# Decay sums of a Mamba-2 scan: spread over the partitions by a DMA through memory, for three chunks in four

## The chip, the cores and the metric

One core of a Trainium2 chip. Its engines are TensorE (PE), VectorE (DVE), ScalarE (ACT), GpSimd (POOL) and SyncE (SP), which here only issues transfers. They run side by side and wait for each other by semaphores. The metric is the time of one execution on the device in microseconds, the median of several.

## The reference

A macaron block on 2048 tokens of width 512: half a feed-forward layer with int4 weights and a low-rank part, a Mamba-2 mixer with a gated feed-forward layer behind it, and again half the feed-forward layer. The change touches the scan of the mixer alone (4 heads of 128, state 128, chunks of 128 tokens):

```python
a = (dt * A).reshape(B, c, Q, H).transpose(0, 1, 3, 2)
cs = jnp.cumsum(a, axis=-1)
Ldec = jnp.where(tri, jnp.exp(cs[..., :, None] - cs[..., None, :]), 0.0)
att = jnp.einsum('bchqn,bchkn->bchqk', Cc, Bc) * Ldec
Yd = jnp.einsum('bchqk,bchkp->bchqp', att, Xdt)
dec_end = jnp.exp(cs[..., -1:] - cs)
Yo = jnp.einsum('bchqn,bchpn,bchq->bchqp', Cc, prev, jnp.exp(cs))
```

`cs`, the decay sums of a chunk, is 4 heads by 128 tokens. It is wanted twice: as a column (a token to a partition) and as a row that is the same on all 128 partitions.

## The kernel before

The program is written out engine by engine; nothing reorders it. There are 16 chunks (`NCH`) of 128 tokens in 4 stretches (`NS`) of 4 (`CH`); chunk c is number j = c mod 4 of stretch i. The middle part, from about 80 to 330 us, runs `step(c)` for c = 0 to 15 on each engine. A step interleaves four things: the first feed-forward layer of chunk c + 8 (`f`, `hi0`, `lo0`, `hi1`, `lo1`, `x1_stats`), the projections and the convolution of the next stretch (`proj`, `slot_a`, `slot_b`, `taps`, `silu`), the scan of chunk c and the first half of that of chunk c + 1, and the output product and residual of chunk c (`w`, `renorm`, `residual2`, `square`). Each stretch has ten projection blocks, dealt out to the steps by `SLOTS = ((0, 1, 2), (3, 4), (5, 6, 7), (8, 9))`.

The scan of a chunk, in the lines of the profile:

- Once a stretch PE forms the sums by a triangular matmul (`csm`, L2022 and L2023), as a column and as rows of 80 partitions in PSUM. DVE (`cut_decay`, L1396 to L1406) takes the negated column into `ncs` and cuts the rows into three bf16 parts in `cs_b`, so that a bf16 matmul gives them back whole.
- For each chunk PE (`s1`) issues four selection matmuls (`decay_rows`, L2047), one a head, which put that head's sums on all 128 partitions, in PSUM bank `B_CS`; then two transposes of x and B (L2041).
- ACT (`scan_ecs`, L817) takes their exponential into `ecs`, copies the transposes into `tm` (`scan1`, L811), and some work later forms the decay matrix (`scan_decay`): four Abs of the row plus the negated column (L826) and an exponential (L829). `scan2` (L835) scales x by `wv`, which DVE makes out of the decay (L1411).
- DVE multiplies decay and product (L1420), POOL masks the triangle and adds the skip (L554, L556), PE multiplies on (`s2_diag` L2066, `s2_state` L2075, `s2_inner` L2083), DVE gates the result (`gate_y`, L1430) and advances the state (L1437), and PE applies the output weights (`w`, L2093).

ACT issues the first half of chunk c + 1 at the start of step c: `scan_ecs`, `scan1`, then convolution blocks and `hi0`, `hi2`, then `scan_decay`, `hi1`, `scan2`. PE's products for the projections and the feed-forward layer share three PSUM banks in turn, each freed by whoever read it last; DVE's `gate_y(c)` frees nothing but is what `w(c)` waits for.

SP's queue is served in order, and an issue whose semaphore isn't there holds up all behind it. Before the loop it does, for c = 4 to 7, the transpose of chunk c's normalised rows (`t1`, L444, which waits for DVE's `lo1(c)`), the load of x for chunk c + 4 (`next_x`, L401) and the transpose for the feed-forward layer (`t0`); then the first pair of gate and up weights (`load_pair`, L436 to L440). In step c it does `t0(c + 9)`, `t2(c - 1)`, `t1(c + 8)`, `next_x(c + 8)`, as far as they exist.

Of the kernel before, what the change touches and what calls it, by code (L numbers as in the profile page):

```python
# [27 lines left out]
def build(nc, x_in, w_in_t, conv_w, conv_b, a_log, d_skip, dt_bias, w_out_t, ln1_w, ln2_w,  # L28
# [23 lines left out]
    with ctx:  # L52
# [209 lines left out]
        e_x_bn, e_x_var, e_x_rstd, e_x_scale, e_n0_hi, e_n0_lo, e_n0_tr = (  # L262
            sem(n) for n in "e_x_bn e_x_var e_x_rstd e_x_scale e_n0_hi e_n0_lo e_n0_tr".split())
        e_n0T, e_ffn, e_x1, e_x1_bn, e_x1_var, e_rms1, e_hn_scale = (
            sem(n) for n in "e_n0T e_ffn e_x1 e_x1_bn e_x1_var e_rms1 e_hn_scale".split())
# [18 lines left out]
        e_scx, e_wscale, e_dsx, e_descale, e_c_var, e_c_rstd, e_c_scale = (  # L284
            sem(n) for n in "e_scx e_wscale e_dsx e_descale e_c_var e_c_rstd e_c_scale".split())
        e_cn_hi, e_cn_lo, e_cffn, e_c_bias, e_out, e_c_bn = (
            sem(n) for n in "e_cn_hi e_cn_lo e_cffn e_c_bias e_out e_c_bn".split())
# [2136 lines left out]
```

## Time and profile before

| | us |
|---|---|
| median of 3 runs | 765.47 |
| lowest and highest | 765.44, 765.92 |
| the profiled execution | 766.1 |
| its span, first to last instruction | 764.4 |
| granted TensorE clock | 1.00 |

An engine's row in a timeline gives the start and the length; "[1.22 <-PE PS L2047]" says that the engine had been idle for 1.22 us and what released it. Matmuls are pipelined and their lengths overlap: what one costs is the distance to the next start. The chain that ended last is followed back from the end, at each step to what released an instruction or to the instruction before it on its engine.

### The profile page before, as it was taken

The numbers are of one execution on the slowest core, as the hardware profiler recorded it, in microseconds if no ns is written. First come the engines' busy times: TensorE is split into PE (matmuls) and PEld (weight loads), VectorE is DVE, ScalarE is ACT, GpSimd is POOL, SyncE is SP. The second block draws the span as 40 slices with busy tenths as digits, with TensorE's granted clock in tenths as the row PEclk, the third lists the DMA queues.
The fourth block names the chain that finished last, engine by engine and source line by source line (L and its number), as shares of the span: only waits on it lengthen the run. The fifth ranks groups of instructions, "written<-read, shape, count | busy, mean of one in ns | idle before, by whom it ended". The sixth has DMA issues, their size and how long they took to land.

```text
span 764.4 us, 10533 instructions
## 1 busy us (share of the span) xinstructions
PE 752.1 (98%) x3406; PEld 351.1 (46%) x3406; DVE 627.6 (82%) x1236; ACT 446.9 (58%) x881; POOL 338.5 (44%) x392
## 2 busy tenths in 40 slices
PE   8999999999999999999999999999999999999998
PEld 3444544454554444444443444444444444444443
DVE  7799778878878979878899978878878878767994
ACT  4867867677786676643645556456456456444441
POOL 5631544663442389765413343243243243224574
PEclk9999999999999999999999999999999999999999
DMA  8833634553331122420520833733733733443564
GB/s 302 198 72 80 148 71 89 107 101 70 69 68 26 33 42 65 87 56 1 137 42 15 179 70 70 165 69 70 166 70 69 164 72 69 79 74 71 120 168 137
DMA packets 95413, 71.85 MB, mean 94 GB/s; under 512 B 65232, under 2 KB 72400, under 8 KB 95360
## 3 DMA queue, kind: packets, MB, share of 16 engines
q0 software_dynamic: 17280, 31.46, 23.0%
q1 hardware_dynamic: 77600, 39.66, 20.1%
q8 instruction: 27, 0.44, 0.2%
q14 instruction: 26, 0.21, 0.1%
q10 hardware_dynamic: 480, 0.07, 0.1%
HBM read 20.32 MB, written 4.19 MB: 32 GB/s over the span
## 4 chain that ended last, share of the span: by engine, by line
PE 66%; DVE 19%; ACT 7%; issue 4%; POOL 2%; DMA 2%; ACTq 0%; POOLq 0%; DVEq 0%
PE PS L1968 59%; PE PS L2093 3%; DVE raw L1455 3%; DVE st L1290 1%; DVE stage L1455 1%; DVE state L1437 1%; DMA x_t<-hb 1%; DVE xs L1387 1%; PE PS L2066 1%; PE PS L2075 1%; ACT pre L885 1%; PE PS L2083 1%; PE PS L2058 1%; ACT raw L886 1%; DVE n_p L1369 1%
## 5 line engine op out<-in xcount | busy, mean ns | idle before, releaser
L713 POOL DMA_DIRECT2D xs<-x x59 | 51.1, 866 | 151.5 <-ACT x L1160 137.5
L1968 PE MATMUL PS<-h,w_in 128*128 128x512 f16 x480 | 108.7, 379 | 0.2 <-issue 0.2
L1968 PE MATMUL PS<-h,x_t 128*128 128x512 f16 x408 | 94.0, 379 | 0.0
L1968 PEld LDWEIGHTS PS<-h,w_in 128*128 128x128 f16 x480 | 46.9, 98 | 65.3 <-issue 15.3
L1968 PE MATMUL PS<-n_T,stage 128*128 128x512 f16 x288 | 71.5, 379 | 0.0
L1160 ACT ACTIVATE x<-PS,d_d 128x512 f32<-128x512 f32 x59 | 40.2, 682 | 39.3 <-PE PS L1968 38.7
L1968 PEld LDWEIGHTS PS<-h,x_t 128*128 128x128 f16 x408 | 39.5, 98 | 48.5 <-issue 2.3
L522 POOL TENSOR_TENSOR r<-mv,mhalf 128x1 f32<-128x1 f32 (+1 forms) x32 | 29.5, 922 | 67.9 <-DVE mv L1294 53.8
L713 POOL DMA_DIRECT2D xs<-n x29 | 25.3, 871 | 70.5 <-ACT n L1160 61.1
L1968 PE MATMUL PS<-pre,stage 128*128 128x512 f16 x192 | 49.3, 379 | 0.0
L1130 ACT ACTIVATE xds<-tm,dgh 128x512 f32<-128x512 f32 x24 | 17.3, 722 | 53.3 <-DVE tm L1897 53.3
L1968 PEld LDWEIGHTS PS<-n_T,stage 128*128 128x128 f16 x288 | 28.2, 98 | 34.0 <-ACT x L1160 0.3
L1968 PE MATMUL PS<-w_ffn,raw_gu 128*128 128x512 f16 x192 | 43.2, 379 | 0.0
L1455 DVE SCALAR_TENSOR_TENSOR raw<-pre,cw,raw 128x512 f32<-128x512 f32 x36 | 28.0, 777 | 9.7 <-ACT raw L886 9.4
L1968 PE MATMUL PS<-raw,x_t 128*128 128x512 f16 x144 | 34.7, 379 | 0.4 <-DVE Ld L1850 0.4
L1968 PE MATMUL PS<-w_in,x_t 128*128 128x512 f16 x144 | 34.8, 379 | 0.0
L1968 PE MATMUL PS<-h,n 128*128 128x512 f16 x144 | 33.2, 379 | 0.3 <-DVE n L1535 0.3
L1160 ACT ACTIVATE n<-PS,d_d 128x512 f32<-128x512 f32 x29 | 19.8, 684 | 23.2 <-PE PS L1968 22.5
L2093 PE MATMUL PS<-w_out,stage 128*128 128x512 f32 x64 | 29.3, 600 | 0.3 <-DVE stage L1430 0.2
L1968 PEld LDWEIGHTS PS<-w_ffn,raw_gu 128*128 128x128 f16 x192 | 18.8, 98 | 22.7 <-DMA raw_gu<-h2n_p 0.3
L1968 PEld LDWEIGHTS PS<-pre,stage 128*128 128x128 f16 x192 | 18.7, 98 | 22.7 <-ACT x L1160 0.3
L2093 PE MATMUL PS<-w_out,raw 128*128 128x512 f32 x64 | 29.0, 595 | 0.1
(319 smaller groups left out, 1821.7 us busy)
## 6 DMA issues: line engine op xcount, KB each, us to landing
xs<-x POOLq DMA_DIRECT2D x75, 256.0 KB, 3.3
xs<-n POOLq DMA_DIRECT2D x29, 256.0 KB, 3.2
x_t<-x_in SPq DMA_DIRECT2D x16, 256.0 KB, 3.0
x_t<-hb POOLq DMA_DIRECT2D x16, 256.0 KB, 3.8
out<-x_t SPq DMA_DIRECT2D x16, 256.0 KB, 2.3
raw_gu<-gate_t SPq DMA_DIRECT2D x7, 512.0 KB, 4.4
raw_gu<-up_t SPq DMA_DIRECT2D x7, 512.0 KB, 6.5
raw_d<-down_t SPq DMA_DIRECT2D x7, 512.0 KB, 7.3
```

Of the source, the lines that this page charges most:

```text
L522: return po.tensor_tensor(dst, src, mhalf[:, 0:src.shape[-1]], ALU.pow)
L713: po.dma_start(chunk_of(xs, c), d_tmps[d % 3], accum_op=ALU.add).then_inc(s_acc[d % 3], 16)
L885: ac.activation(pre[:, w, NTAP - 1:], src, ACT.Copy)
L886: last = ac.activation(xbc[i % 2][:, b, :], src, ACT.Identity, scale=cw[:, b, NTAP - 1:NTAP], bias=cb[:, b:b + 1])
L1130: ac.activation(th_s[ab], u4 if ab else c11, ACT.Tanh, scale=dgh[:, p % 2:p % 2 + 1]).then_inc(e_tanh_g, 1)
L1160: ac.activation(d_tmps[d % 3], bank(d_bank(d)), ACT.Copy, scale=d_d[:, p % 3:p % 3 + 1]).then_inc(e_ev, 1)
L1290: link(ve.bn_stats(stat, src), e_link, base + 1)
L1369: return ve.tensor_tensor(pair_[:, 1, :], src, pair_[:, 0, :], ALU.subtract)
L1387: link(ve.scalar_tensor_tensor(chunk_of(xs, c), bank(b), 0.5 / ACT_SCALE if c < NF else d_f[:, :], x_t[:, j, :], ALU.mult, ALU.add), e_x1, ...
L1455: ins = ve.scalar_tensor_tensor(xbc[i % 2][:, b, :], pre[:, w, k:k + ST], cw[:, b, k:k + 1], xbc[i % 2][:, b, :], ALU.mult, ALU.add)
L1968: ins = pe.matmul(out_, lhs(a, b, k), rhs(a, b, k), start=first and n == 0, stop=last and n == len(todo) - 1)
L2093: last = pe.matmul(bank(b), y[:, h, (c % CH) * P:(c % CH + 1) * P], w_out[:, h, :], start=h == 0, stop=h == H - 1)
```

## The change

For chunks with j = 1, 2 and 3 the row on all partitions comes from memory. DVE copies the 16 rows of a stretch as they are in PSUM into `cs_f` (first thing in `cut_decay`); SP writes them to a tensor `cs_d` in memory (`cs_store`) and for each such chunk reads the 512 numbers back, the same for every partition, into one buffer `cs_all` (`cs_rows`). ACT's `scan_ecs` and `scan_decay` read `cs_all` in SBUF for these chunks and wait for the transfer. For j = 0 the selection matmuls stay. `cs_all` is free for chunk c when the Abs of the chunk that used it before are done (`e_gap`). In the last three steps `t2(c - 1)` moves behind `cs_rows`. To make room for semaphores, pairs that followed each other on one engine now count on that engine's common semaphore (`chain` in place of `link`); these instructions and their order stay.

```diff
+        cs_f = sb("cs_f", [CH * H, P])
+        cs_all = sb("cs_all", [P, H, P])
+        cs_d = nc.dram_tensor("cs_d", (NS, CH, 1, H * P), F32, kind="Internal").ap()
...
+            def cs_store(i):
+                sp_.wait_ge(e_cs_f, i + 1)
+                sp_.dma_start(cs_d[i, :, 0, :].rearrange("j (h t) -> (j h) t", h=H), cs_f[:, :]).then_inc(s_csd, 16)
+
+            def cs_rows(c):
+                i, j = divmod(c, CH)
+                if j > 0:
+                    sp_.wait_ge(s_csd, (i + 1) * 16)
+                    if c > 1:
+                        sp_.wait_ge(e_gap, c if j > 1 else c - 1)
+                    sp_.dma_start(cs_all[:, :, :].rearrange("p h t -> p (h t)"), cs_d[i, j, :, :].broadcast_to([P, H * P])).then_inc(s_cs, 16)
...
+                if c == CH + 1:
+                    cs_store(0)
+            cs_rows(1)
             sp_.wait_ge(e_cv, NPC)
             load_pair(0)
...
-                if c > 0:
+                if 0 < c <= 3 * CH:
                     t2(c - 1)
                 if a < NCH:
                     t1(a)
                     next_x(a)
+                if c + 2 < NCH:
+                    cs_rows(c + 2)
+                if c % CH == 2 and c + 2 < NCH:
+                    cs_store(c // CH + 1)
+                if c > 3 * CH:
+                    t2(c - 1)
...
+            def rows_ready(c, j):
+                if j == 0:
+                    ac.wait_ge(e_cs, c // CH + 1)
+                else:
+                    ac.wait_ge(s_cs, (c - c // CH) * 16)
+
+            def rows_of(j):
+                return cs_all[:, :, :] if j else heads(B_CS)
...
-                ac.wait_ge(e_cs, c + 1)
+                rows_ready(c, j)
                 if c - 1 > 0:
                     ac.wait_ge(e_state, c - 1)
-                ac.activation(ecs[:, j % 2, :, :], heads(B_CS), ACT.Exp).then_inc(e_ecs, 1)
+                ac.activation(ecs[:, j % 2, :, :], rows_of(j), ACT.Exp).then_inc(e_ecs, 1)
...
                     ve.wait_ge(e_cs_col, i + 1)
+                    if i > 0:
+                        ve.wait_ge(s_csd, i * 16)
+                    ve.tensor_copy(cs_f[:, :], rows[0:NT]).then_inc(e_cs_f, 1)
                     ve.tensor_copy(cs_b[0:K_CS, :], rows[0:K_CS]).then_inc(e_cs_cut, 1)
...
                 if j == 0:
                     pe.wait_ge(e_cs_b, i + 1)
-                if c > 0:
-                    pe.wait_ge(e_gap, c)
-                decay_rows(B_CS, j).then_inc(e_cs, 1)
-                if j == 0:
+                    if c > 0:
+                        pe.wait_ge(e_gap, c - CH + 1)
+                    decay_rows(B_CS).then_inc(e_cs, 1)
                     pe.wait_ge(e_xbc, i * CB + 2)
...
-            def stats(src, mv, stat, e_link, base, e_ve):
-                link(ve.bn_stats(stat, src), e_link, base + 1)
-                link(ve.bn_aggr(mv[:, 0:2], stat), e_link, base + 2)
+            def stats(src, mv, stat, e_ve):
+                chain(ve.bn_stats(stat, src))
+                chain(ve.bn_aggr(mv[:, 0:2], stat))
```

On SP, where the loop is entered (from the transpose of chunk 6's rows on; `h` is the tensor that the transposes fill, x_t the loads of x), before:

```order
L444 DMA_TRANSPOSE h<-hn_p 128x8x128 [waits e_hn_lo]
L401 DMA x_t<-x_in 128x512 [waits e_x1]
L444 DMA_TRANSPOSE n_T<-n_p 128x8x128 [waits e_ffn,e_n0_lo]
L444 DMA_TRANSPOSE h<-hn_p 128x8x128 [waits e_hn_lo]
L401 DMA x_t<-x_in 128x512 [waits e_x1]
L436 DMA raw_gu<-gate_t 128x4x256 [waits e_cv]
L437 DMA raw_gu<-up_t 128x4x256
L440 DMA raw_d<-down_t 128x2x512
L444 DMA_TRANSPOSE n_T<-n_p 128x8x128 [waits e_ffn,e_n0_lo]
```

and now:

```order
L470 DMA cs_d<-cs_f 16x128 [waits e_cs_f]
L447 DMA_TRANSPOSE h<-hn_p 128x8x128 [waits e_hn_lo]
L404 DMA x_t<-x_in 128x512 [waits e_x1]
L447 DMA_TRANSPOSE n_T<-n_p 128x8x128 [waits e_ffn,e_n0_lo]
L447 DMA_TRANSPOSE h<-hn_p 128x8x128 [waits e_hn_lo]
L404 DMA x_t<-x_in 128x512 [waits e_x1]
L478 DMA cs_all<-cs_d 128x512 [waits s_csd]
L439 DMA raw_gu<-gate_t 128x4x256 [waits e_cv]
L440 DMA raw_gu<-up_t 128x4x256
L443 DMA raw_d<-down_t 128x2x512
L447 DMA_TRANSPOSE n_T<-n_p 128x8x128 [waits e_ffn,e_n0_lo]
```

The store of the first stretch's sums stands first in this piece; the read of chunk 1's rows stands behind the last transpose and load ahead of the loop, and the weight pair follows it.

On ACT, in step 0, from the last product of the prologue to the decay of chunk 1, before:

```order
L901 ACTIVATE th<-PS,d_ih 128x512 [waits e_proj,e_sz]
L817 ACTIVATE ecs<-PS 128x512 [waits e_cs]
L811 ACTIVATE tm<-PS 128x256 [waits e_xB_tr]
L768 ACTIVATE n<-x_t,b,r 128x512 [waits s_n0T,e_x_scale]
L768 ACTIVATE n_p<-x_t,b,r 128x512
L826 ACTIVATE Ld<-PS,ncs 128x128 [waits e_S,e_cs,e_ncs]
L826 ACTIVATE Ld<-PS,ncs 128x128 x3
L829 ACTIVATE Ld<-Ld 128x512 [waits e_gap]
```

and now:

```order
L930 ACTIVATE th<-PS,d_ih 128x512 [waits e_proj,e_sz]
L846 ACTIVATE ecs<-cs_all 128x512 [waits s_cs]
L831 ACTIVATE tm<-PS 128x256 [waits e_xB_tr]
L788 ACTIVATE n<-x_t,b,r 128x512 [waits s_n0T,e_x_scale]
L788 ACTIVATE n_p<-x_t,b,r 128x512
L855 ACTIVATE Ld<-cs_all,ncs 128x128 [waits e_S,s_cs,e_ncs]
L855 ACTIVATE Ld<-cs_all,ncs 128x128 x3
L858 ACTIVATE Ld<-Ld 128x512 [waits e_gap]
```

Nothing moved; the exponential and the Abs read another buffer and wait for a transfer in place of PE.

On PE, around `s1(2)`, between the projection blocks of step 0 and the feed-forward product of step 1, before:

```order
L1968 MATMUL PS<-h,w_in 128x512 [waits e_conv]
L1968 MATMUL PS<-h,w_in 128x512 x11
L2047 MATMUL PS<-cs_b,sel_b 128x128 [waits e_gap]
L2047 MATMUL PS<-cs_b,sel_b 128x128 x3
L2041 MATMUL PS<-ident,stage 128x128 [waits e_spx,e_xB_T]
L2041 MATMUL PS<-ident,stage 128x128
L1968 MATMUL PS<-w_ffn,n_T 128x512 [waits e_x2,s_n0T]
L1968 MATMUL PS<-w_ffn,n_T 128x512 x11
L2066 MATMUL PS<-S,tm 128x512 [waits e_y,e_xB_T,e_SD]
```

and now:

```order
L2000 MATMUL PS<-h,w_in 128x512 [waits e_conv]
L2000 MATMUL PS<-h,w_in 128x512 x11
L2072 MATMUL PS<-ident,stage 128x128 [waits e_spx,e_xB_T]
L2072 MATMUL PS<-ident,stage 128x128
L2000 MATMUL PS<-w_ffn,n_T 128x512 [waits e_x2,s_n0T]
L2000 MATMUL PS<-w_ffn,n_T 128x512 x11
L2096 MATMUL PS<-S,tm 128x512 [waits e_y,e_xB_T,e_SD]
```

Four matmuls are gone from between the blocks; the same at the other eleven chunks with j > 0.

## Rows read from the trace of the kernel before

**Rows 1.** The page: busy us by engine; share of the chain by engine.

```profile
PE 752.1 (98%) x3406; PEld 351.1 (46%) x3406; DVE 627.6 (82%) x1236; ACT 446.9 (58%) x881; POOL 338.5 (44%) x392
...
PE 66%; DVE 19%; ACT 7%; issue 4%; POOL 2%; DMA 2%; ACTq 0%; POOLq 0%; DVEq 0%
```

**Rows 2.** Chain that ended last, 55 to 345 us: start, length in us, what.

```profile
106.13 0.68 ACT raw L886
...
147.31 3.70 PE PS L2093 x8
...
173.91 0.68 ACT stage L886
...
281.63 1.12 PE PS L2066 x2
```

**Rows 3.** Selection matmuls: line 2047 by form, then PE's timeline (start, length).

```profile
L2047 PE MATMUL PS<-cs_b,sel_b x64: 217/218/222, 79.2 to 306.5; 80*128 80x128 bf16 x64
...
119.75 0.39 PE L2047 MATMUL PS<-cs_b,sel_b 80*128 80x128 bf16 x4
...
119.97 0.39 PE L2041 MATMUL PS<-ident,stage 128*128 128x128 f32 x2
```

**Rows 4.** SP's timeline, 60 to 340 us: start, time of issue.

```profile
85.88 1.23 SPq L444 DMA_TRANSPOSE h<-hn_p  x1
...
87.16 1.06 SPq L401 DMA_DIRECT2D x_t<-x_in  x1
...
152.25 0.57 SPq L401 DMA_DIRECT2D x_t<-x_in  x1
```

**Rows 5.** DMA issues, KB, us to landing: 88 to 90 us; page; hb's load.

```profile
raw_gu<-gate_t SPq DMA_DIRECT2D x1, 512.0 KB, 4.4
...
x_t<-x_in SPq DMA_DIRECT2D x1, 256.0 KB, 3.6
...
x_t<-x_in SPq DMA_DIRECT2D x16, 256.0 KB, 3.0
...
DMA to landing us min/median/max: 5.7/5.7/5.7
```

**Rows 6.** ACT's timeline: start, length, [idle before <-releaser].

```profile
86.55 0.58 ACT L817 ACTIVATE ecs<-PS 128x512 f32<-128x512 f32 x1
...
92.41 0.81 ACT L788 ACTIVATE hn<-xs,b,r 128x512 f32<-128x512 f32 x1 [1.92 <-POOL b L525]
...
101.86 0.21 ACT L884 ACTIVATE pre<-hist 128x3 f32<-128x3 f32 x1 [0.27 <-PE PS L1968]
...
104.68 0.60 ACT L817 ACTIVATE ecs<-PS 128x512 f32<-128x512 f32 x1 [1.22 <-PE PS L2047]
...
154.60 0.59 ACT L817 ACTIVATE ecs<-PS 128x512 f32<-128x512 f32 x1
...
160.71 0.82 ACT L788 ACTIVATE hn<-xs,b,r 128x512 f32<-128x512 f32 x1 [1.55 <-POOL b L525]
```

**Rows 7.** DVE's timeline around chunk 1, and PE's row of its w.

```profile
97.08 2.33 DVE L1455 SCALAR_TENSOR_TENSOR raw<-pre,cw,raw 128x512 f32<-128x512 f32 x3 [0.67 <-ACT raw L886]
...
103.26 0.75 DVE L1455 SCALAR_TENSOR_TENSOR raw<-pre,cw,raw 128x512 f32<-128x512 f32 x1 [1.82 <-ACT raw L886]
...
106.83 0.75 DVE L1455 SCALAR_TENSOR_TENSOR raw<-pre,cw,raw 128x512 f32<-128x512 f32 x1 [1.17 <-ACT raw L886]
...
112.82 0.74 DVE L1430 SCALAR_TENSOR_TENSOR stage<-PS,d_ih,stage 128x512 f32<-128x512 f32 x1
...
113.62 3.70 PE L2093 MATMUL PS<-w_out,stage 128*128 128x512 f32 x8
```

**Rows 8.** Lines 1396 and 829 by form; PE's longest wait, 55 to 335 us.

```profile
L1396 DVE CAST cs_b<-PS x4: 276/277/281, 62.2 to 263.8; 80x128 bf16<-80x128 f32 x4
...
L829 ACT ACTIVATE Ld<-Ld x16: 629/630/632, 82.3 to 310.6; 128x512 f32<-128x512 f32 x16
...
PE PS L2066 <- POOL S L556: 1.0, 1, 1.0
```

More of the change, by code:

```diff
@@ L261, in build @@
         e_aexp = sem("e_aexp"); e_wf = sem("e_wf"); e_dve = sem("e_dve"); e_pool = sem("e_pool")
[L262 to L265, printed above, removed]
+        e_x_var, e_x_scale, e_n0_hi, e_n0_lo, e_n0_tr = (
+            sem(n) for n in "e_x_var e_x_scale e_n0_hi e_n0_lo e_n0_tr".split())
+        e_n0T, e_ffn, e_x1, e_x1_var, e_hn_scale = (
+            sem(n) for n in "e_n0T e_ffn e_x1 e_x1_var e_hn_scale".split())
         e_hn_hi, e_hn_lo, e_proj, e_conv, e_hist = (
@@ L283, in build @@
             sem(n) for n in "e_gated_lo e_down e_acc e_w_gu0 e_w_gu1d e_w_hi e_fold e_mk".split())
[L284 to L287, printed above, removed]
+        e_scx, e_wscale, e_descale, e_c_var, e_c_scale = (
+            sem(n) for n in "e_scx e_wscale e_descale e_c_var e_c_scale".split())
+        e_cn_hi, e_cn_lo, e_cffn, e_c_bias, e_out, = (
+            sem(n) for n in "e_cn_hi e_cn_lo e_cffn e_c_bias e_out".split())
         W_HI_G = [4 * p - 1 for p in range(NP)]
@@ L528, in ln0 @@
                 po.wait_ge(e_x_var, c + 1)
-                rsqrt(r0[:, c:c + 1], mv0[:, c, 2:3]).then_inc(e_x_rstd, 1)
-                po.wait_ge(e_x_rstd, c + 1)
+                chain(rsqrt(r0[:, c:c + 1], mv0[:, c, 2:3]))
                 shift(b0[:, c:c + 1], r0[:, c:c + 1], mv0[:, c, 0:1]).then_inc(e_x_scale, 1)
@@ L540, in ln1_chain @@
                 po.wait_ge(e_x1_var, c + 1)
-                rsqrt(r1[:, c, :], mv1[:, c, 2:4]).then_inc(e_rms1, 1)
-                po.wait_ge(e_rms1, c + 1)
+                chain(rsqrt(r1[:, c, :], mv1[:, c, 2:4]))
                 shift(b1[:, c, :], r1[:, c, :], mv1[:, c, 0:1]).then_inc(e_hn_scale, 1)
@@ L732, in c_norm @@
                 po.wait_ge(e_c_var, c + 1)
[L733 to L734 removed]
+                chain(rsqrt(rC[:, c:c + 1], mvC[:, c, 2:3]))
                 shift(bC[:, c:c + 1], rC[:, c:c + 1], mvC[:, c, 0:1]).then_inc(e_c_scale, 1)
@@ L825, in scan_decay @@
                 for h in range(H):
-                    last = ac.activation(Ld[:, h, :], heads(B_CS)[:, h, :], ACT.Abs, bias=ncs[:, s, j * H + h:j * H + h + 1])
+                    last = ac.activation(Ld[:, h, :], rows_of(j)[:, h, :], ACT.Abs, bias=ncs[:, s, j * H + h:j * H + h + 1])
                 last.then_inc(e_gap, 1)
@@ L2042, in s1, with decay_rows @@
                 last.then_inc(e_xB_tr, 1)
-            def decay_rows(b, j):
+            def decay_rows(b):
                 for h in range(H):
-                    n = j * H + h
-                    last = pe.matmul(heads(b)[:, h, :], sel_b[0:K_CS, n:n + 1].broadcast_to([K_CS, P]), cs_b[0:K_CS, :],
+                    last = pe.matmul(heads(b)[:, h, :], sel_b[0:K_CS, h:h + 1].broadcast_to([K_CS, P]), cs_b[0:K_CS, :],
                                      start=True, stop=True)
```

23 lines of the change are left out of this document (10 added, 13 removed).

## The prediction

> **What bounds the kernel now.** I read the page's busy line and chain first [rows 1]. TensorE (PE) is busy 98% of the span, so time taken from it looks like time won; but only 66% of the chain of work that ended last is PE, 19% is VectorE (DVE) and 7% ScalarE (ACT). So the next view is the chain in order of time for the stretch of the scan, 80 to 330 us [rows 2]. It leaves PE a little before 106.13, runs through DVE and ACT until w of chunk 3 starts at 147.31, is PE again until ACT's piece at 173.91, and then stays off PE until 281.63, where the diagonal product of chunk 12 waits for a result of GpSimd (POOL). PE hardly idles there, since two loops run nearly level: PE's matmuls, and the DVE/ACT chain of taps, statistics and gates that feeds it. Whatever makes PE alone faster is given back at the next place where it meets the other loop. These meeting points (w of chunk 1 at 113.62 [rows 7], w of chunk 3, the products of chunks 8, 12 and 14) decide the sum; the last views are the timelines around them, and that of the sync queue (SP), which is to issue the new transfers.
>
> **Removed: selection matmuls.** 64 stood in the program, at 218 ns each by the profile [rows 3]. That duration overlaps: the four of chunk 3 start at 119.75 and the next work at 119.97, so a group takes 0.22 us of PE's time. Three groups in four go: 12 x 0.22 = 2.7 us. This is the most the change can win on PE, 0.35% of the run. It is on the path only where PE is the later loop.
>
> **Removed: a wait of ACT for PE.** The exponentials of chunk 2 wait 1.22 us for the selection matmuls and only then, 0.5 us later, the copy of the transposes starts; chunk 6 repeats this at 172.46 [rows 6]. With the rows from memory the exponential fits into that wait, if they are there: 0.22 (PE is done earlier) + 0.48 (the exponential no longer ahead of the copy) = 0.7 us off the ACT chain, twice. Elsewhere ACT doesn't wait for these matmuls, and nothing is won.
>
> **Added: a copy on DVE,** 16 x 128 from PSUM, four times, ahead of the cast to cs_b. The nearest row is that cast, 277 ns for 80 x 128 [rows 8], of which some 0.2 us is the step to the next instruction. The first, at 62 us, lies ahead of the scan and is covered by a wait of DVE for ACT of some 0.4 us; the other three are in DVE's chain: 0.2 us at each, 0.6 in all.
>
> **Added: ACT reads SBUF in place of PSUM** for 12 chunks. The exponential from PSUM takes 0.58 us [rows 6], that from SBUF 0.63 [rows 8]; with the four Abs some 0.2 us a chunk as an upper bound, zero as a lower. ACT has idle time at most of these places, so I put 0.1 us on the path in all, beside what I count at chunk 1.
>
> **Added: 12 transfers of 256 KB and 4 of 8 KB.** Bandwidth is no concern: 3.1 MB beside 71.85 MB. Their place in SP's queue is. The rows of chunk 1 are issued behind the transpose that waits for DVE (issued at 85.88) and the load of x behind it (87.16, taking 1.06 of SP's time) [rows 4], so at 88.22. ACT wants them for the exponential at 86.55 [rows 6]: they are late before they are issued. The store ahead of them is long done (the sums are cut at 62 us). How long until they land: the load of the same size just ahead, issued at 87.16, landed in 3.6 us [rows 5]; the weights of 512 KB behind it in 4.4; the one broadcast of this shape, hb, in 5.7 with several loads ahead of it. The median of the x loads is 3.0, and I see nothing below it but by a tenth. I take 3.6, as the nearest in time, size and queue. So the rows are there at 91.8, and ACT starts 5.3 us late.
>
> By the Trainium skill (DMA: Bandwidth & Descriptors, the section on the cost of a DMA) a transfer costs some 2.0 us fixed plus its bytes over 436 GB/s, which for 256 KB would be 2.6 us, an estimate; the trace shows 3.6, not this. With 2.6 the sum below would be 1.0 us smaller. The same page advises to issue a transfer early and wait late, which speaks against this place in the queue.
>
> **What becomes of those 5.3 us.** Behind the exponential on ACT stand the normalisation of chunk 9, the decay of chunk 1, the normalisation of chunk 8 and the first convolution, whose result DVE takes at 97.08 [rows 7].
> 1. From 86.55 to 97.08 ACT waits 1.92 us for POOL [rows 6]; the late start swallows this. Work: 10.53 - 1.92 = 8.6, with SBUF reads 8.8. DVE's taps start at 91.8 + 8.8 = 100.6, 3.5 late.
> 2. To the taps of the next block (103.26) it is 6.18 us of taps, residual, square and convolution, with 0.27 of waiting for PE [rows 6] that goes: 100.6 + 5.9 = 106.5, 3.3 late.
> 3. The three taps take 2.4 us (2.33 in the merged row of 97.08, and small steps). DVE is free at 108.9. In the trace it idled 1.17 us there and went on at 106.83 [rows 7]: 2.1 late.
> 4. Thence DVE is busy without a gap to the gate of chunk 1 (112.82), for which w of chunk 1 waits; it starts at 113.62 + 2.1. What PE saved on chunks 1 and 2 (0.45) is lost in this wait.
> 5. Up to 147.31 the chain is DVE/ACT: + 2.1 + 0.2 for the copy = + 2.3. Chunk 3's saving is swallowed; its rows come in time, since SP issues them some 5 us before ACT wants them and both move alike.
> 6. From 147.31 PE leads: - 0.45 for chunks 5 and 6. The rows of chunk 5 are issued at 152.25 + 0.57 + 2.3 = 155.1 [rows 4] and land at 158.1 to 158.7 (3.0 to 3.6 us); ACT wants them at 154.60 + 2.3 = 156.9. That is 1.2 to 1.8 late, but ACT had 1.55 us of waiting for POOL behind it, before 160.71 [rows 6], which takes up nearly all. At chunk 6 the exponential leaves the chain: - 0.48. So + 1.4.
> 7. From 173.91 to 281.63 the chain is off PE; the savings of chunks 7, 9, 10 and 11 turn into longer waits there (the one of 1.0 us for POOL [rows 8] grows). + 0.2 + 0.2 for two copies: + 1.8. Rows 7, 9, 10, 11, 13 and 14 come in time by the same count; those of chunk 15 queue behind a weight pair and may be 1 to 2 us late, into idle time of ACT.
> 8. + 0.1 for reads from SBUF; chunks 14 and 15 save PE time that it waits off at the product of chunk 14: **+ 1.9 us.**
>
> The profiled execution lies at 766.1 (span 764.4 and 1.7 around it), 0.6 above the median of 765.47. The sum was made in it, and would give 768.0; on the median, **767.4**. Landing in 3.0 us takes 0.6 off (766.8). At 4.4 the first lateness grows by 0.8 and the second, past its cover, by about 0.9: 769.1.
>
> **Rivals.**
> - *The rows come in time, or the lateness finds cover I don't see.* For it: ACT is 58% busy. Against it: 88.22 against 86.55. Then steps 1 to 3 turn to - 0.75, + 0.2 for the copy is - 0.55 at w of chunk 3; chunks 5 and 6 bring it to - 1.3; the copies and SBUF reads leave - 0.8: 764.7, no difference. Chance 0.23.
> - *PE's saving is all real.* The DVE/ACT chain would have slack that the view doesn't show, since PE idles so little: 765.47 - 2.7 = 762.8. Against it: off PE from 173.91 to 281.63. Chance 0.07.
> - *Slower yet: the broadcast is a slow kind of transfer.* 128 reads of one row of memory, landing like hb in 5.7: the first lateness adds 2.1 to my figure; chunk 5 then comes at 162.8, 4 past its cover, and chunk 9 misses too: some + 7, 772 to 773. It decides from about 4.5 us of landing on, where the loss at chunk 5 starts to count in full. Chance 0.10.
> - *My own case,* + 1.2 to + 3.7: chance 0.60. A part of it, some 0.13, lies within 0.2%.
>
> **Numbers.** About 0.2% (1.5 us) is what a measurement of this kernel can tell from no change. Slower by more: 0.47 of my case and 0.10: 0.57. Within: 0.13 and 0.23: 0.36. Faster: 0.07. The range of 8 in 10 takes in my case with its bounds and the first rival, with 0.3 us more below and 0.9 above, since DVE instructions here are at times 1 us longer than their like and may fall otherwise: 764.4 to 770.0.
>
> **What the profile after would show.** ACT idle before the exponential of chunk 1, some 5 us, released by a DMA; its start near 91.8. The landing time of the transfers to cs_all: 3.0 to 3.7. DVE idle longer before the taps at 97 us; w of chunk 1 some 2 us later than 113.62, released by DVE. PE with 48 matmuls fewer but no less time at 281.63. ACT not idle for a DMA at chunks 2, 3, 6, 7; a second wait of 1 to 2 us at chunk 5. I am wrong if SP issues the first transfer before 86 us, if PE's wait at w of chunk 1 doesn't grow, or if the distance between chunk 8's product and chunk 12's shrinks, which would say that PE led there.

## The result, and the profile after

The changed kernel took 770.46 us as the median of five executions (769.45 to 772.13), the kernel before 765.66 (765.44 to 765.97, five): a ratio of 1.0060, 95% interval 1.0047 to 1.0073. It is slower, as forecast, but by 4.8 us where 1.9 was forecast, and 770.46 lies outside the range of 764.4 to 770.0.

The profiled execution took 769.58 us, with a span of 767.8 (before: 766.1 and 764.4). So 3.4 us of the loss stand in the traces. The rest lies between the executions: the median of before is 0.4 under its profiled execution, that of after 0.9 above.

The page of the changed kernel, busy us and the shares of the chain, to be held against [rows 1]:

```profile
PE 749.7 (98%) x3358; PEld 348.8 (45%) x3358; DVE 627.8 (82%) x1240; ACT 448.7 (58%) x881; POOL 336.7 (44%) x392
...
PE 56%; DVE 24%; ACT 9%; issue 5%; DMA 4%; POOL 1%; SPq 0%; ACTq 0%; DVEq 0%; POOLq 0%
```

PE has 48 matmuls fewer and 2.4 us less to do, and its share of the chain falls from 66% to 56%; DMA's rises from 2% to 4%. In the scan it shows in the chain in order of time, 80 to 165 us (start, length, what):

```profile
85.89 1.23 SPq L447
87.17 0.58 SPq L404
87.79 4.92 DMA cs_all<-cs_d
93.64 0.70 ACT n L788
...
154.25 1.21 POOL S L578
155.45 4.95 DMA x_t<-hb
160.51 0.76 DVE xs L1416
```

Two transfers are on it. The first is the rows of chunk 1. The second is a transfer that is in the kernel before too: POOL's addition of `hb` to a chunk of x. SP's timeline and then ACT's show the first, and the two other places where ACT waits for rows (chunks 5 and 15):

```profile
85.89 1.23 SPq L447 DMA_TRANSPOSE h<-hn_p  x1
87.17 0.58 SPq L404 DMA_DIRECT2D x_t<-x_in  x1
87.79 0.43 SPq L478 DMA_DIRECT2D cs_all<-cs_d  x1
...
155.66 0.36 SPq L478 DMA_DIRECT2D cs_all<-cs_d  x1
```

```profile
92.73 0.63 ACT L846 ACTIVATE ecs<-cs_all 128x512 f32<-128x512 f32 x1 [6.08 <-DMA cs_all<-cs_d]
...
159.10 0.63 ACT L846 ACTIVATE ecs<-cs_all 128x512 f32<-128x512 f32 x1 [1.69 <-DMA cs_all<-cs_d]
...
313.18 0.63 ACT L846 ACTIVATE ecs<-cs_all 128x512 f32<-128x512 f32 x1 [1.22 <-DMA cs_all<-cs_d]
```

DVE's timeline has the taps behind chunk 1's exponential (before, in [rows 7]: 97.08, 103.26, 106.83) and the residual that waits for `hb`; then PE's row of the gated output of chunk 1 (before: 113.62):

```profile
101.43 2.33 DVE L1487 SCALAR_TENSOR_TENSOR raw<-pre,cw,raw 128x512 f32<-128x512 f32 x3 [1.25 <-ACT raw L915]
...
107.22 0.75 DVE L1487 SCALAR_TENSOR_TENSOR raw<-pre,cw,raw 128x512 f32<-128x512 f32 x1 [1.44 <-ACT raw L915]
...
109.55 0.74 DVE L1487 SCALAR_TENSOR_TENSOR raw<-pre,cw,raw 128x512 f32<-128x512 f32 x1
...
160.51 0.75 DVE L1416 SCALAR_TENSOR_TENSOR xs<-PS,d_f,x_t 128x512 f32<-128x512 f32 x1 [2.37 <-DMA x_t<-hb]
```

```profile
116.33 3.70 PE L2123 MATMUL PS<-w_out,stage 128*128 128x512 f32 x8 [2.08 <-DVE stage L1462]
```

The lateness falls from 6.18 us at ACT (92.73 against 86.55) over 4.35, 3.96 and 2.72 at the taps to 2.71 at the gated output, and there it stays.

**How the runs below are compared.** The same row is looked up in each trace, and its start in the kernel before is taken off. Five places do: ACT's exponential of chunk 1 (86.55 before), of chunk 2 (104.68) and of chunk 7 (192.38), PE's diagonal product of chunk 12 (281.63), and the whole span (764.4). All in us, minus is earlier:

| kernel | chunk 1 | chunk 2 | chunk 7 | chunk 12 | span | median, us |
|---|---|---|---|---|---|---|
| after | +6.18 | +2.65 | +2.72 | +3.14 | +3.4 | 770.46 |
| e1 rows of chunk 1 early | -0.14 | -2.11 | -1.17 | -0.75 | -0.8 | 765.89 |
| e2 also those of 5, 9, 13 | +0.31 | -1.21 | -1.13 | -0.72 | -0.4 | 765.58 |
| e3 no transport | +0.44 | -1.05 | -0.95 | -0.72 | -0.7 | 765.37 |
| e4 transport beside the matmuls | -0.5 | -0.5 | -0.1 | 0.0 | -0.1 | 766.52 |
| e5 after, again | +5.96 | +2.43 | +2.78 | +3.26 | +4.1 | 770.10 |
| e6 only 5, 9, 13 early | +6.88 | +3.35 | +3.68 | +4.09 | +4.6 | 769.47 |
| e7 hb early | +8.11 | +4.57 | +5.67 | +7.37 | +7.3 | 772.76 |
| e8 rows of chunk 1 behind the weights | +12.34 | +8.81 | +9.05 | +9.28 | +9.3 | 775.28 |
| e9 weights wait for the rows | +5.69 | +2.15 | +2.30 | +2.78 | +2.8 | 770.83 |
| e10 chunk 1 by matmuls | +0.22 | -1.16 | -0.40 | +0.08 | +0.1 | 765.97 |
| e11 as e2, and 15 early | -0.16 | -1.66 | -1.54 | -1.08 | -1.1 | 765.21 |
| e12 no transport, from PSUM | +1.87 | +0.02 | +0.12 | +0.07 | 0.0 | 765.52 |
| e14 busy wait | +6.16 | +2.63 | +2.71 | +3.17 | +3.2 | 770.12 |
| e15 after, once more | +6.62 | +3.09 | +3.25 | +3.71 | +4.6 | 770.25 |

The kernel before had medians of 766.33 beside e1 to e4, 765.92 beside e5 to e8, 766.05 beside e9 to e12 and 765.95 beside e13 to e15. The traces of e7, e8 and e12 begin the scan 1.9 to 2.1 us late already (chunk 0). They are 1.5 us behind 10 us from the start, which none of these edits touches; why is open. That much is to be taken off e7's and e8's rows, and a good part of it (it stands 1.45 later than e3 at chunk 0 and 0.8 later at chunk 12) off e12's. The ratios, but not the medians, leave out one execution each of e8, e13 and e14 that ran far above the rest (2816, 789 and 4556 us; without it the medians are 775.14, 769.56 and 770.04), and e13 has no row since its was the traced one, at a mean clock of 0.949.

### The profile page after: what moved, and what is told of

Its sections match the earlier page's. It is cut to its first block, busy times and chain, and to the rows that moved or that the text cites. A ratio compares the mean times of both kernels' runs of the same rounds, so it can differ in the third digit from the quotient of the medians.

```text
span 767.8 us, 10471 instructions
## 1 busy us (share of the span) xinstructions
PE 749.7 (98%) x3358; PEld 348.8 (45%) x3358; DVE 627.8 (82%) x1240; ACT 448.7 (58%) x881; POOL 336.7 (44%) x392
## 4 chain that ended last, share of the span: by engine, by line
PE 56%; DVE 24%; ACT 9%; issue 5%; DMA 4%; POOL 1%; SPq 0%; ACTq 0%; DVEq 0%; POOLq 0%
PE PS L2000 52%; DVE raw L1487 3%; DVE stage L1487 2%; DMA x_t<-hb 2%; DVE state L1469 1%; PE PS L2131 1%; DVE st L1319 1%; DMA raw_d<-down_t 1%; DVE S L1452 1%; ACT xds L864 1%; DVE xs L1416 1%; PE PS L2123 1%; ACT pre L914 1%; DVE x L1478 1%; ACT raw L915 1%
## 5 line engine op out<-in xcount | busy, mean ns | idle before, releaser
L576 POOL TENSOR_SCALAR_AFFINE_SELECT S<-S 128x512 f32<-128x512 f32 x16 | 15.3, 953 | 32.4 <-DVE S L1452 32.4
```

The costliest lines, as they stand in the source:

```text
L576: chain(po.affine_select(out=S[:, j % 2, :, :], in_=S[:, j % 2, :, :], compare_op=ALU.is_ge, fill=0.0, base=0, pattern=[[0, H], [1, P]], c ...
```

## Is it the rows of chunk 1? (e1 to e4)

My theory after the result: the whole loss is the one late transfer. Its rival: the transport costs by being there (copies, traffic, reads from SBUF). e1 issues the rows of chunk 1 one step earlier, behind the transpose of chunk 8:

```diff
+                if c == CH + 2:
+                    cs_rows(1)
-            cs_rows(1)
```

> Changed kernel, with the read of chunk 1's rows issued right after the transpose for chunk 8's feed-forward layer (near 80 us) in place of near 88 us. Nothing else moves. Theory (the late first rows are the cost): the 6.1 us that ACT waits before chunk 1's exponential go, all that follows moves some 3 us earlier, and the time is about that of the kernel before, 765.0 to 766.3. Rival (the 16 transfers and their contention cost the time, wherever they stand): at most 1 us better than the changed kernel, 769 to 770.

Measured: 765.89 us (11 executions), ratio 0.9996, 0.9986 to 1.0007. The loss is gone. SP's row, the landing and ACT's exponential of e1:

```profile
80.33 0.58 SPq L478 DMA_DIRECT2D cs_all<-cs_d  x1
...
86.41 0.62 ACT L847 ACTIVATE ecs<-cs_all 128x512 f32<-128x512 f32 x1
```

Here ACT doesn't wait, and the span is 4.2 us shorter than that of after with one line moved. At chunk 6, though, e1 wins nothing. ACT still waits 1.9 us for the rows of chunk 5, and DVE for `hb`:

```profile
156.63 0.75 DVE L1417 SCALAR_TENSOR_TENSOR xs<-PS,d_f,x_t 128x512 f32<-128x512 f32 x1 [2.49 <-DMA x_t<-hb]
```

e2 moves the rows of chunks 5, 9 and 13 to the head of their step as well, ahead of the transposes.

```diff
+                if (c + 2) % CH == 1 and c + 2 < NCH:
+                    cs_rows(c + 2)
...
-                if c + 2 < NCH:
+                if c + 2 < NCH and (c + 2) % CH > 1:
```

> As e1_first_early, and the rows of chunks 5, 9 and 13 too are issued at the head of their step of the sync queue, ahead of two transposes and a load of x. Theory (chunk 5 is late too, and its transfer, issued beside the accumulation of hb into x for chunk 12, makes that one land late): ACT's wait of 1.7 us for chunk 5's rows goes, DVE's first sum of chunk 12 no longer waits for hb, and the time is 0.7 to 1.3 us below e1: 764.0 to 765.2. Rival (chunk 5's lateness lies in idle time of ACT, as predicted, and hb's landing scatters by itself): the same as e1 within 0.4 us.

Measured: 765.58 us, ratio 0.9989, 0.9979 to 0.9999. ACT's wait is gone. DVE's wait before that residual is 1.3 us, as long as it was for PE in the kernel before, though it is `hb` that ends it even now. From chunk 3 to chunk 7 the lateness goes from -0.40 to -1.13: 0.7 of the 0.93 us that step 6 of the prediction counted on are there when the rows are. In e1 it goes from -1.29 to -1.17 over the same stretch, in after from +2.72 to +2.72. The time doesn't show it: 0.3 under e1 is what the rival expected, not the theory's 0.7 to 1.3. The trace of e1 was 0.9 ahead of e2's at chunk 3 by other causes, and at chunk 12 the two are level. So this gain stands on one stretch of the traces.

e3 leaves out the transport, a part of what is to be computed: for three chunks in four ACT reads a constant of the same shape in SBUF.

```diff
-                return cs_all[:, :, :] if j else heads(B_CS)
+                return d_diag[:, :, :] if j else heads(B_CS)
```

> The changed kernel without the copy, the store and the reads: ACT takes the rows of chunks with j > 0 from a constant tile in SBUF, so the row term of the decay is left out for these chunks (the column stays). It bounds what taking away 48 matmuls can give. Theory (two level loops, the saving of PE is mostly given back at waits for DVE): 1.0 to 1.6 us below the kernel before, 764.0 to 764.7. Rival (PE bounds, all of 2.7 us is real): 762.5 to 763.2.

Measured: 765.37 us, ratio 0.9993, 0.9984 to 1.0002, above the 764.0 to 764.7 expected. With 48 matmuls gone and nothing in their place the kernel gains nothing that can be measured. PE's 2.7 us are not to be had here at any price of the transport.

e4 is the kernel before with copies, stores and reads added, for which nobody waits.

```diff
+                    ve.tensor_copy(cs_f[:, :], rows[0:NT]).then_inc(e_cs_f, 1)
...
+                if c + 2 < NCH:
+                    cs_rows(c + 2)
```

> The kernel before with the copy, the store and the twelve reads added in the changed kernel's places, while PE still makes the rows of all chunks and ACT still reads them in PSUM; nobody but the next read waits for the transfers. Theory (latency counts, traffic doesn't): 0.4 to 0.8 us of copies on DVE and up to 1 us where hb lands later beside chunk 5's transfer: 766.0 to 767.4. Rival (traffic and the sync queue's time are the cost): 768.5 to 770.5, as the changed kernel.

Measured: 766.52 us, ratio 1.0005, 0.9996 to 1.0013. The traffic alone costs nothing that shows in the time, but DVE's wait before the residual doubles, from 1.3 us for PE to 2.6 for `hb`. The row of e4:

```profile
157.55 0.75 DVE L1415 SCALAR_TENSOR_TENSOR xs<-PS,d_f,x_t 128x512 f32<-128x512 f32 x1 [2.60 <-DMA x_t<-hb]
```

The `hb` addition landed in 3.8 us before, where SP's load of x (256 KB) is issued half a microsecond ahead of it, and in 5.2 here, where SP's read of the rows (256 KB) follows 0.2 us behind as well. With nobody waiting for the rows, this wait makes e4 only 0.2 us later from chunk 5 to chunk 7.

e10 replaces the late rows in another way: chunk 1 takes its rows from matmuls, the other eleven from memory.

```diff
+                if c == 1:
+                    pe.wait_ge(e_gap, 1)
+                    decay_rows(B_CS, 1).then_inc(e_cs, 1)
```

> The changed kernel, but chunk 1 takes its rows from selection matmuls on PE, as before; the other eleven chunks still take them from memory. If the late rows of chunk 1 are the whole of the loss, the time is that of the kernel with these rows issued early: 765.6 to 766.2, within 0.1% of the kernel before, and the diagonal product of chunk 12 lies 0.6 to 0.8 us earlier than before. If the other transfers, the copies or the rows of chunks 5, 9 and 15 cost something too, 767 or more.

Measured: 765.97 us beside 766.05, ratio 1.0001, 0.9992 to 1.0009. The time is as expected; at chunk 12 it is level with before instead of 0.7 earlier. With the rows of chunk 5 still late, chunk 6's gain is missing (-0.32 at chunk 4, -0.40 at chunk 7), and the copies and reads take it to +0.08.

## How much of a lateness comes through (e5, e6, e8)

e5 is the changed kernel again.

> The changed kernel itself, once more, beside the three below. Theory: 769.4 to 771.0, ACT waiting about 6 us for chunk 1's rows and everything from chunk 2 on about 2.7 us later than before. Rival (the two times of 772 were the rule and a third cause adds 2 us in most executions): a median above 771.5.

Measured: 770.10 us, ratio 1.0056, 1.0042 to 1.0071.

e6 moves the rows of chunks 5, 9 and 13 as e2 does, and leaves those of chunk 1 late.

> The changed kernel, with the rows of chunks 5, 9 and 13 issued at the head of their step of the sync queue; chunk 1's stay late. Theory (chunk 5's lateness beyond ACT's idle time, and hb landing later beside it, swallow what PE saves on chunks 5 and 6): the shift against the kernel before falls from + 2.7 us at chunk 5 to about + 1.7 at chunk 6, and the time is 0.7 to 1.1 us below e5. Rival (DVE's chain has no slack for PE's saving here at all): + 2.7 stays at chunk 6, the time is that of e5.

Measured: 769.47 us, ratio 1.0043, 1.0030 to 1.0055, 0.6 under e5 where 0.7 to 1.1 was expected; the two intervals overlap. Its trace gains less than e2's at chunk 6 (+3.41 at chunk 3, +3.03 at chunk 6) and loses it again by chunk 7; the section on the clock returns to it.

e8 issues the rows of chunk 1 behind the three weight loads.

```diff
-            cs_rows(1)
             sp_.wait_ge(e_cv, NPC)
             load_pair(0)
+            cs_rows(1)
```

> The changed kernel, with the read of chunk 1's rows issued behind the first pair of gate and up weights (1.5 MB) in place of ahead of it: the lateness is enlarged. Theory (each us that these rows are later costs 1 us): they land 3 to 4.5 us later than in e5, ACT's wait before chunk 1's exponential is 9 to 11 us, and the time rises by as much, 773.0 to 775.0. Rival (part of the lateness is taken up by idle time of DVE further on): under 2 us above e5.

Measured: 775.28 us, ratio 1.0118, 1.0103 to 1.0132. That is just above the 773.0 to 775.0 expected. ACT's row of e8, which stands 6.2 us behind that of after (its wait is 4.1 us longer, the rest is the late start):

```profile
98.89 0.63 ACT L846 ACTIVATE ecs<-cs_all 128x512 f32<-128x512 f32 x1 [10.17 <-DMA cs_all<-cs_d]
```

Put side by side in the table, chunk 1 and chunk 2 say how much is covered: 6.18 becomes 2.65, 5.96 becomes 2.43, 6.88 becomes 3.35, 12.34 becomes 8.81. It is 3.53 us each time, in e9, e14 and e15 too. So, held against the kernel before, a lateness of 3.5 us would break even, and between 5.7 and 12.3 us every further one counts in full; no run has these rows between 1 and 5 us late. Not all of the 3.5 is idle time of ACT and DVE. With the rows in time the kernel gets ahead of the one before by itself: from chunk 1's exponential to its gated output the shift goes from -0.14 to -1.29 in e1, from +0.31 to -0.40 in e2, from -0.16 to -0.84 in e11. Held against such a kernel only some 2.3 to 2.8 us are free. After crossed the 3.5 by 2.7.

## Why they land so late (e9, e13)

3.6 us of landing were forecast. Measured at this place: 4.9 in after, 4.6, 5.2 and 5.5 in e5, e14 and e15 (4.6 to 5.5 in all nine traces that have it at 87 to 90 us), against 3.3 in e1, some 7 us earlier in the run. Two neighbours are near: the load of x ahead, and 1.5 MB of weights behind. In e9 the weights wait until the rows have landed.

```diff
             cs_rows(1)
             sp_.wait_ge(e_cv, NPC)
+            sp_.wait_ge(s_cs, 16)
             load_pair(0)
```

> The changed kernel, but SP waits until the rows of chunk 1 have landed before it issues the three weight loads of 512 KB that stood right behind them. Theory A (the 4.9 us of landing, where 3.6 was forecast, come from sharing the DMA engines with those 1.5 MB): the rows land in 3.2 to 3.7 us, ACT's wait before the exponential of chunk 1 falls from 6.1 to 4.5 to 5.0 us, and as every microsecond of it counts in full, the kernel gains 1.1 to 1.6 us on the change: near 768.8, still 2.5 to 3.5 above the kernel before. The weights land some 4 us later and nobody waits for them. Theory B (it is the kind of transfer, 128 reads of one row of memory, or the load of x just ahead of it): landing stays at 4.6 to 5.0, and the time at 770.

Measured: 770.83 us, ratio 1.0065, 1.0052 to 1.0077, no gain. SP's timeline of e9 and the landing, in us:

```profile
87.00 0.58 SPq L404 DMA_DIRECT2D x_t<-x_in  x1
87.62 0.43 SPq L478 DMA_DIRECT2D cs_all<-cs_d  x1
92.28 0.38 SPq L439 DMA_DIRECT2D raw_gu<-gate_t  x1
```

```profile
DMA to landing us min/median/max: 4.6/4.6/4.6
```

The weights leave some 4 us later, and the rows land in 4.6 as in e5 with the weights behind them. Theory A fell.

e13 issues the rows ahead of the load of x.

```diff
+                if c == 2 * CH - 1:
+                    cs_rows(1)
                 next_x(c)
...
-            cs_rows(1)
```

> The changed kernel, but SP issues the rows of chunk 1 ahead of the load of x, at 87.0 in place of 87.8; the load of x and the weights come behind it. Theory A (the load of x just ahead takes the first share of the DMA engines): the rows land in 3.3 to 3.8 us, ACT's exponential of chunk 1 starts at 90.4 to 90.9 in place of 92.6, and the kernel gains 1.6 to 2.2 us: 767.9 to 768.6. Theory B (the kind of transfer, or the transpose ahead): landing stays at 4.6 to 4.9, and the gain is the earlier issue alone, 0.6 to 0.8: near 769.5.

Measured: 769.62 us beside 770.25 of e15, ratio to before 1.0043, 1.0031 to 1.0055: 0.6 us better, which is what the earlier issue gives by itself. From its trace only the landing is read: 4.6 us. Theory A (the load of x ahead) fell too. Neither neighbour alone explains the 1.3 us over e1. Beside e1's rows there was no load of x at all, in e9 and e13 always one, ahead or behind, and no run leaves out both neighbours at this place. But a load of 256 KB beside the rows isn't enough to make them slow. The rows of chunk 2 in after have one 0.7 us ahead, and POOL's addition of `hb` 0.2 us ahead. SP's and POOL's timelines, and the landing:

```profile
100.47 0.58 SPq L404 DMA_DIRECT2D x_t<-x_in  x1
101.15 0.38 SPq L478 DMA_DIRECT2D cs_all<-cs_d  x1
```

```profile
100.96 0.92 POOL L560 DMA_DIRECT2D x_t<-hb  x1
```

```profile
DMA to landing us min/median/max: 3.6/3.6/3.6
```

Those of chunks 3 and 5, with the same neighbours, land in 3.6 and 3.4, and over all traces every read of rows but those of chunk 1 near 88 us and those behind the weights landed in 3.0 to 4.3. Nor are the DMA engines full while ACT waits. In e9, stretches of 1 us (DMA share and GB/s last):

```profile
89.00:90.00 1.00, 1.00 (x10) 0.96 (x9) 0.93 (x3) 0.00 (x0) 0.00 (x0) 1.00 0.99 367
90.00:91.00 1.00, 1.00 (x3) 0.38 (x2) 0.16 (x2) 0.00 (x0) 0.71 (x1) 1.00 0.13 43
91.00:92.00 1.00, 1.00 (x5) 0.38 (x4) 0.00 (x0) 0.00 (x0) 0.27 (x1) 1.00 0.04 12
```

The bulk had moved by 90, and the last two microseconds of the wait are for a few packets. In after, e6, e14 and e15, the four traces with the longest landings (4.9 to 5.5), a packet of the DMA queue that the profile calls instruction took 1.7 to 2.3 us of this time, mostly 0.9 to 1.5 elsewhere. Which held up which isn't shown, and in e5 (4.6) it began only 4.0 us behind the issue. What holds the rows up near 88 us, and only there, stays open.

## A second transfer, moved (e7, e11, e12)

In e7 POOL issues the addition of `hb` one step ahead, before its share of the scan, so that it and the rows of chunk 5 don't meet.

```diff
+                if a + 1 < NCH:
+                    xb(a + 1, (a + 1) % CH)
                 if c + 1 < NCH:
                     scan_c(c + 1, (c + 1) % CH)
                     scan_d(c + 1, (c + 1) % CH)
-                if a + 1 < NCH:
-                    xb(a + 1, (a + 1) % CH)
```

> The changed kernel, with POOL issuing the accumulation of hb into x (for chunk c + 9) ahead of its two scan pieces of step c and not behind them, some 4 us earlier. Theory: DVE's first sum of chunk 12 waits for PE instead of for hb, but ACT's lateness at chunk 5 remains, so about half of the 1 us of e6 comes: 0.3 to 0.7 us below e5. Rival (hb's landing alone holds the chain): as much as e6 or more. Rival (it is of no matter): the same as e5, or slower by the 0.9 us that POOL's scan pieces start later.

Measured: 772.76 us, ratio 1.0087, 1.0074 to 1.0100, slower by 2.7 than e5, some 2 of it from the late start of its trace, if the other executions had that too. POOL's timeline of e7 shows what else it did:

```profile
153.46 0.92 POOL L560 DMA_DIRECT2D x_t<-hb  x1
154.08 1.60 POOL L572 TENSOR_TENSOR raw<-raw,ecs 128x512 f32<-128x512 f32 x1
156.82 1.02 POOL L576 TENSOR_SCALAR_AFFINE_SELECT S<-S 128x512 f32<-128x512 f32 x1 [1.14 <-DVE S L1452]
```

The issue takes 0.9 us of POOL. The triangle (`S`, L576) starts 5.3 us after POOL's inverse roots of that step (151.54); in after it is 4.3 (153.14 and 148.81). DVE's residual now waits 0.29 us, and for PE. That PE waits for the later triangle instead isn't shown: the diagonal product of this step starts without a wait, and from 80 to 330 us PE waits for the triangle 2.6 us in e7 and 2.5 in after. Where e7 loses what its late start doesn't explain stays open; all three expectations missed.

e11 is e2 with the rows of chunk 15 ahead of the second weight pair.

> The changed kernel with the rows of chunks 1, 5, 9 and 13 issued at the head of their step, and those of chunk 15 ahead of the second weight pair. ACT no longer waits 1.2 us for the rows of chunk 15. My theory says that nobody waits for ACT there, since POOL leads at the products of chunks 12 to 15: no gain over the kernel without the last move, 765.3 to 765.8, 0 to 0.6 us under the kernel before. If the wait of ACT counted, 764.4 to 764.8.

Measured: 765.21 us beside 766.05, ratio 0.9991, 0.9982 to 0.9999. No gain over e2 that can be told: ACT's wait at chunk 15 was into idle time, as step 7 had it. It is the best version of this idea, 0.8 us or 0.1% under the kernel before, within what counts as no change.

e12 leaves out the transport as e3 does (all four chunks of a stretch use the rows of its first), but reads PSUM.

> Leaves out a part of the computation: no copy, store or transfer of the decay sums, and all four chunks of a stretch use the rows of its first chunk, read from PSUM. Against the kernel without transport that reads SBUF it prices the reads from SBUF alone. The prediction put 0.1 us of them on the path and at most 0.2 us a chunk (2.4 in all). By the 0.1: 765.2 to 765.6, the same as with SBUF reads. By the upper bound: 763.0 to 763.5. If 2.7 us of PE's time could be won at all, it would have to show here: 762.7.

Measured: 765.52 us, ratio 0.9991, 0.9980 to 1.0001; with SBUF reads it was 765.37. Between chunk 7 and chunk 12 e3 loses 0.23 us and e12 none, so reads from SBUF may cost some 0.3 there; that rests on one trace each, and e12's had a late start to make good. The upper bound of 2.4 us was far off.

## Why the median is above the profile (e14, e15)

The traces of e5 and e15 show two things that the trace of after doesn't.

**A lateness that grows behind the scan.** At 440 to 460 us PE waits for DVE's largest value of a weight tile. The wait in after, then in e5, then in e15 (us in total, times, longest), 345 to 545 us:

```profile
PE PS L2164 <- DVE mx L1519: 0.5, 1, 0.5
```

```profile
PE PS L2164 <- DVE mx L1519: 1.1, 2, 0.6
```

```profile
PE PS L2164 <- DVE mx L1519: 1.3, 2, 0.7
```

It is 0.5 before too. In e5 and e15 there is a second wait, and +3.3 and +3.8 at the end of the scan are +4.1 and +4.6 of span. But this is not a threshold of lateness: e7 and e8, which leave the scan 7.4 and 9.3 us late, have the one wait of 0.5 us and don't grow, and e2, which leaves it early, has two (0.7 in all). What sets the second wait stays open.

**The granted clock.** In e5 PE idles 2.09 us before the gated output of chunk 1 and then runs it in 5.40 us instead of 3.70; in e15 the same happens at chunk 0 after 1.55 us. First e5, then e15:

```profile
116.11 5.40 PE L2123 MATMUL PS<-w_out,stage 128*128 128x512 f32 x8 [2.09 <-DVE stage L1462]
```

```profile
96.96 5.37 PE L2123 MATMUL PS<-w_out,stage 128*128 128x512 f32 x8 [1.55 <-issue]
```

Stretches of 1 us of e5 (stretch, width, busy us of PE, PEld, DVE, ACT, POOL, granted clock, DMA share, GB/s):

```profile
116.00:117.00 1.00, 0.89 (x2) 0.38 (x3) 1.00 (x2) 1.00 (x2) 0.99 (x1) 0.66 0.42 97
117.00:118.00 1.00, 1.00 (x3) 0.48 (x2) 1.00 (x4) 0.31 (x1) 0.00 (x0) 0.50 0.74 165
118.00:119.00 1.00, 1.00 (x3) 0.48 (x2) 1.00 (x6) 0.32 (x2) 0.00 (x0) 0.50 0.24 56
119.00:120.00 1.00, 1.00 (x2) 0.30 (x2) 1.00 (x4) 1.00 (x5) 0.24 (x1) 0.63 0.93 207
120.00:121.00 1.00, 1.00 (x4) 0.46 (x3) 0.96 (x3) 1.00 (x3) 0.92 (x2) 1.00 0.00 0
```

The clock is at its lower level, 1.2 in place of 2.4 GHz, for some 3.4 us. After and e9 have the same idle time (2.08) and no fall, so such idle time does not always bring one. Over the executions it goes with the lateness: a mean clock of 0.998 or less had 6 of 17 of the changed kernel, 4 of 6 of e9, and 12 of the 13 of e6, e7 and e8; none of the 84 of before beside these runs, and none of the 77 of e1 to e4 and e10 to e12. The six executions of the changed kernel at 0.998 or less have a median of 771.4 us, the other eleven 769.8. Which of the two, the clock or a longer lateness, is the cause there isn't shown, and one of 773.43 ran at 0.999. What a fall costs is less plain. In e5 the gated output of chunk 3 is 1.1 us later than its DVE input and PE is behind for a while; from chunk 2 to chunk 12 e5 loses 0.83 where after loses 0.49. In e6 the same fall may have eaten the gain of chunk 6: DVE waits 1.34 us for PE there. So some 0.3 us in e5, an estimate from one trace each. e14 fills the idle time with four matmuls whose result is overwritten.

```diff
+                if c == 1:
+                    pe.wait_ge(*freed)
+                    for n in range(4):
+                        pe.matmul(bank(b), ident[:, :], w_out[:, n, :], start=True, stop=True)
                 pe.wait_ge(e_y, c + 1)
```

> The changed kernel with four extra matmuls of 128x512 (their result is overwritten) on PE ahead of the gated output of chunk 1, into PE's idle 2.1 us; they take some 1.85 us. Of the changed kernel's 11 executions so far 4 had a mean granted clock of 0.998, of the kernel before none. Theory A (PE's clock falls after this idle time, and that makes the executions of 772 us): the clock is 0.999 or 1.0 in all executions, the highest time falls from 773 to under 771, and the median by 0.3 to 0.8 us, to 769.3 to 769.9. Theory B (the clock costs nothing that the DVE/ACT chain doesn't hide, or falls elsewhere): median 770.1 to 770.5, highest again 772 or more.

> The changed kernel again, beside the two: median 770.1 to 770.5, highest 772 to 773, and a clock of 0.998 in about four executions of ten.

Measured: 770.12 us for e14 (ratio 1.0050, 1.0037 to 1.0064), 770.25 for e15 (1.0055, 1.0037 to 1.0072); a clock of 0.998 in 1 execution of 5 and in 2 of 6. Theory A wanted none, and a highest time under 771; it was 771.94. I had mis-sized the filling: it took 3.6 us, not 1.85, and made PE 1.2 late at the gated output, which chunk 6 took up. So it doesn't settle what the clock costs; in the executions of 772 us and more, of which no trace was taken, that stays open.

## Why the prediction was right in sign and wrong in size

- **What bounds the kernel** was right. e3 and e12 take the matmuls away for nothing and gain 0.5 to 1.0 us against the kernel before beside them, not 2.7; the rival "PE's saving is all real" (762.8) is refuted, and the rival "the rows come in time" with its -0.8 is what e1, e2, e3 and e11 show (-0.7 to -1.1 at chunk 12). Its own sum had a slip: -0.55 with 0.93 off at chunks 5 and 6 is -1.5 and not -1.3, so that it should have ended at -1.0.
- **Issue and landing: the first failed term.** SP was free at 87.79, 0.4 earlier than counted (the load of x took 0.58 of it, not 1.06). But the rows landed in 4.92 where I took 3.6. I took one row, the load of x just ahead, and had 4.4 and 5.7 beside it; that same load landed in 2.9 in the trace of after. Together +0.9: ACT was 6.2 late, not 5.3. 3.6 is what the rows of chunk 2 took; why those of chunk 1 take 4.6 to 5.5 stays open. The rival of a slow broadcast set its threshold at 4.5 us of landing and 772. The first landing is past that, but its mechanism did not come: the rows of chunk 5 landed in 3.4, ACT's lateness there found its cover as step 6 has it, and ACT didn't wait for those of chunk 9.
- **Steps 1 to 4** predicted 3.2 us of cover, 3.5 it was (the same in every trace with late rows): -0.3. The taps came at 101.43, 107.22 and 109.55 where 100.6, 106.5 and 108.9 were forecast, the gated output of chunk 1 at +2.71 for +2.1.
- **Step 5**, a copy for 0.2: the lateness doesn't move (+2.71 to +2.73 at the gate of chunk 3). -0.2.
- **Step 6: the second failed term.** -0.93 was counted for chunks 5 and 6, 0.0 came (+2.72 at chunk 3, +2.68 at chunk 6). The rows of chunk 5 were late by 1.69, within the forecast, but I looked only for ACT's cover. The same step has `hb`, issued by POOL at 155.45, 0.2 us from SP's read at 155.66; it landed in 4.95 in place of 3.8, and DVE waited 2.37 us for it, where in the kernel before it waits 1.26 for PE. I had weighed the new transfers against the length of SP's queue and not against the other engines' transfers in flight. In the chain that ended last it is `hb` that stands there, not the rows. In e2, where neither is late, 0.7 of the 0.93 come. What each of the two costs by itself no run tells: e2 and e6 move both, e4 has the late `hb` alone and loses 0.2, and e7's loss isn't explained.
- **Steps 7 and 8** hold: +0.5 forecast from chunk 7 to the end of the scan, +0.46 measured (2.72 to 3.18). The sum 1.9 + 0.9 - 0.3 - 0.2 + 0.9 is the 3.2 at the end of the scan.
- **Beyond the scan** I took the lateness as carried to the end unchanged. It grows by 0.2 in after and by 0.8 in e5 and e15, which have a second wait for DVE's largest value near 446 us; these two profiled executions (770.18 and 770.80) lie where the medians do, that of after (769.58) under them. So 4.8 against 1.9 is 1.3 of these two terms and the rest of the scan, 0.2 behind the scan, and some 1.3 between a traced execution and a median (the traced one of before lies 0.4 above its median, that of after 0.9 under), which no run explains in full.

By the Trainium skill (DMA: Bandwidth & Descriptors, the section Anatomy of one DMA) 256 KB would take 2.6 us, an estimate by its fixed part and rate, which it gives for transfers that GpSimd issues, while the rows are issued by SP; no read of the rows here landed in under 3.0. The advice of the Trainium skill (the same page, Rules for kernel authors) to issue early and wait late agrees with e1: 7.5 us earlier was worth 4.2.

## What to carry to other kernels

Before an engine's work is moved to a transfer, look up when its issuing queue gets to it and when the reader wants it; a single first transfer that comes too late can cost more than all the later ones save, and the cure is one line. Price its landing by the spread of such rows and not by one of them, since the same read landed in 3.3 to 5.5 us here, and ask what the loss is at the upper end. Price as well what the new transfer does to those of other queues. Time taken from the busiest engine is worth nothing while another chain runs level with it: leaving the work out altogether is the cheap way to learn that first.
